# A first group loaded in parts, and a masked maximum taken in one pass: a graph attention layer with pre-normalisation on one core

## The reference

```python
def reference(x, adj, Wq, bq, Wk, bk, Wv, bv, beta):       # x 64x128x384, adj 64x128x128, W 384x384
    h = maximum(layernorm(x), 0)
    q, k, v = heads(h @ Wq + bq), heads(h @ Wk + bk), heads(h @ Wv + bv)      # 12 heads of 32
    scores = q @ k.T / sqrt(32) + beta * adj
    scores = where(adj > 0, scores, -9e15)
    return x + merge(softmax(scores) @ v)
```

## Time and profile before

| | us |
|---|---|
| median of 3 runs | 582.98 (582.75 to 583.28) |
| the profiled execution, its own time | 582.67 |
| its span, first to last instruction | 580.9 |
| PE busy | 552.8 (95%) |
| DVE busy | 469.2 (81%) |
| ACT busy | 464.4 (80%) |
| POOL busy | 115.6 (20%) |

### The profile page before, as it was taken

One profiled execution on the slowest core, in us unless ns is written; L12 is line 12 of the kernel. 1 busy time (PEld: TensorE's weight loads), 2 busy tenths in 40 slices (PEclk: granted clock), 3 DMA queues, 4 the chain that ended last, 5 costly groups with the idle time before them and its releaser, 6 DMA issues.

```text
span 580.9 us, 16356 instructions
## 1 busy us (share of the span) xinstructions
PE 552.8 (95%) x5664; PEld 470.1 (81%) x5664; DVE 469.2 (81%) x803; ACT 464.4 (80%) x1861; POOL 115.6 (20%) x200
## 2 busy tenths in 40 slices
PE   1999999999999999999999999999999999999873
PEld 1778888888888888888888888888888888888662
DVE  5778898888888888889888888988888898777771
ACT  4258889888888988888888888888888889887884
POOL 2201211222121121222112112221211212111111
PEclk9999999999999999999999999999999999999997
DMA  8120120300212020021202112120211200000001
GB/s 287 47 74 16 46 82 16 101 29 32 81 45 68 27 92 35 32 81 42 71 27 80 44 34 81 37 76 27 67 46 45 81 32 30 28 29 29 15 33 37
DMA packets 28429, 31.71 MB, mean 55 GB/s; under 512 B 2544, under 2 KB 28400, under 8 KB 28400
## 3 DMA queue, kind: packets, MB, share of 16 engines
q1 hardware_dynamic: 28400, 31.34, 16.4%
HBM read 18.75 MB, written 12.58 MB: 54 GB/s over the span
## 4 chain that ended last, share of the span: by engine, by line
PE 92%; DVE 2%; issue 2%; ACT 1%; POOLq 0%; POOL 0%
PE G_ps L503 35%; PE S_ps L564 18%; PE PT_ps L548 15%; PE S_ps L523 10%; PE PT_ps L534 8%; PE S_ps L574 3%; PE PT_ps L554 3%; DVE probs L438 2%; ACT probsT L297 1%; ACT probs L289 0%; POOLq L44 0%; DVE h_lo L372 0%; POOL y L264 0%; DVE qk L401 0%; DVE y L448 0%
## 5 line engine op out<-in xcount | busy, mean ns | idle before, releaser
L289 ACT ACTIVATE probs<-probs,negmax 128x128 f32<-128x128 f32 x768 | 298.4, 401 | 0.0
L297 ACT COPY probsT<-PT_ps 128x512 f32<-128x512 f32 x192 | 111.9, 587 | 83.6 <-PE PT_ps L548 81.9
L289 ACT ACTIVATION_READ_ACCUMULATOR probs<-probs,negmax 128x1 f32 x768 | 153.2, 200 | 0.0
L264 POOL TENSOR_TENSOR y<-y,x_ring 128x384 f32<-128x384 f32 x64 | 65.2, 1019 | 312.7 <-DVE y L448 312.7
L503 PE MATMUL G_ps<-h_hi,w_hi 128*128 128x512 f32 x288 | 118.6, 412 | 3.1 <-DVE h_lo L372 3.1
L548 PE MATMUL PT_ps<-ident,probs 128*128 128x128 f32 x768 | 117.5, 277 | 2.5 <-ACT probs L289 1.7
L503 PE MATMUL G_ps<-h_hi,w_lo 128*128 128x512 f32 x288 | 118.5, 411 | 0.0
L503 PE MATMUL G_ps<-h_lo,w_hi 128*128 128x512 f32 x288 | 117.2, 407 | 0.0
L452 DVE TENSOR_REDUCE negmax<-probs 128x12 f32<-128x1536 f32 x64 | 111.6, 1743 | 0.1
L438 DVE TENSOR_TENSOR probs<-S_ps,bias 128x1536 f32<-128x1536 f32 x64 | 109.1, 1705 | 2.2 <-PE S_ps L523 2.2
L548 PEld LDWEIGHTS PT_ps<-ident,probs 128*128 128x128 f32 x768 | 88.1, 140 | 13.0 <-ACT probs L289 3.2
(11 more groups left out here) (36 smaller groups left out, 617.0 us busy)
## 6 DMA issues: line engine op xcount, KB each, us to landing
x_ring<-in_x_dram SPq DMA_DIRECT2D x16, 768.0 KB, 4.7
out_dram<-y SPq DMA_DIRECT2D x64, 192.0 KB, 1.8
adj_in<-in_adj_dram SPq DMA_DIRECT2D x16, 256.0 KB, 2.8
w_raw<-in_L_gnn_Wq_dram SPq DMA_DIRECT2D x1, 576.0 KB, 5.7
w_raw<-in_L_gnn_Wk_dram SPq DMA_DIRECT2D x1, 576.0 KB, 6.7
w_raw<-in_L_gnn_Wv_dram SPq DMA_DIRECT2D x1, 576.0 KB, 7.8
bv_rows<-in_L_gnn_bv_dram SPq DMA_DIRECT2D x1, 192.0 KB, 6.8
bq_raw<-in_L_gnn_bq_dram SPq DMA_DIRECT2D x1, 1.5 KB, 7.1
```

The source lines that it names most:

```text
L264: nc.gpsimd.tensor_tensor(y[:, z.s % 2, :], y[:, z.s % 2, :], x_ring[:, bass.ds(at, D)], ALU.add).then_inc(y_ready, 1)
L289: last = nc.scalar.activation(p, p, ACT.Exp, bias=negmax[:, e, j * KC + m:j * KC + m + 1], accum_out=rowsum[:, e, m * HC + j:m * HC + j + 1])
L297: nc.scalar.copy(probsT[:, m, :], PT_ps[:, m % 2, :]).then_inc(pT_stored[m], 1)
```

## The change

Group 0's x comes in four DMAs, Wq in two (the first 128 columns ahead of the third graph), and Wk and Wv are issued behind the constants and group 1's x. The rounded copies and remainders of the weights are made by unit; all remainders but the first unit's are made on POOL. On DVE a graph's normalisation stands after the next graph's moments. `low_part` of the slots with T but no P stands ahead of `moments`. PE multiplies the identity by itself into a free bank ahead of each of the first transposes. In the slots with P but no A, PE's `transpose_xhat` stands at the end of the slot. The scores, the mask term and beta change sign, so that the mask and the negated maximum become one instruction per head, twelve to a graph, with y after them; `values` waits for the first three of them, `transpose_xhat` for the first six.

```diff
+TURN = -1.0
+MASK_ORDER = [1, 0, 2, 3]
+WARM = [8, 2, 2, 2, 4]
@@ SP
-            sp.dma_start(x_ring[:, 0:GROUP * D].rearrange("p (s d) -> p s d", s=GROUP), x_v[:, 0, :, :]).then_inc(x_loaded[0], 16)
-            for c, w in enumerate((wq, wk, wv)):
-                sp.dma_start(w_raw[:, :, c * D:(c + 1) * D], w.rearrange("(k p) n -> p k n", p=P)).then_inc(w_loaded[c], 16)
+            for q in range(2):
+                load_first(q)
+            load_weights(0, wq, 0, P, w_first)
+            for q in range(2, GROUP):
+                load_first(q)
+            load_weights(0, wq, P, D, w_loaded[0])
...
             sp.dma_start(x_ring[:, GROUP * D:2 * GROUP * D].rearrange("p (s d) -> p s d", s=GROUP), x_v[:, 1, :, :]).then_inc(x_loaded[1], 16)
+            load_weights(1, wk, 0, D, w_loaded[1])
+            load_weights(2, wv, 0, D, w_loaded[2])
@@ POOL
+            def weights_low(first, last):
+                pool.wait_ge(w_hi_ready, min(last, QK_UNITS + 1))
+                ws = slice(first * P, last * P)
+                nc.gpsimd.tensor_tensor(w_lo[:, :, ws], w_raw[:, :, ws], w_hi[:, :, ws].bitcast(F32), ALU.subtract).then_inc(w_lo_ready, 1)
...
+                    weights_low(1, 2)
+                    weights_low(2, 3)
+                if z.static and z.P and z.groups(0) == 0:
+                    if z.s < GROUP - 1:
+                        weights_low(KC + z.s, KC + z.s + 1)
+                    else:
+                        weights_low(QK_UNITS, 3 * KC)
@@ ACT
-                    act.wait_ge(negmax_ready, z.e + 1)
+                    act.wait_ge(masked, z.e + 1)
...
-                    last = nc.scalar.activation(p, p, ACT.Exp, bias=negmax[:, e, j * KC + m:j * KC + m + 1],
+                    last = nc.scalar.activation(p, p, ACT.Exp, bias=negmax[:, e, j * KC + m:j * KC + m + 1], scale=TURN,
@@ DVE
-                        for w in group:
-                            normalise(w)
-                        weights_low(0)
+                            if w.s > 0:
+                                normalise(group[w.s - 1])
+                        normalise(group[-1])
+                        first_weights_low()
...
-                    nc.vector.tensor_tensor(probs[:, a, :, :, :], S_ps[:, :, 0:KC * N].rearrange("p j (m k) -> p j m k", m=KC),
-                                            bias[(z.par + 1) % 2][:, z.s, :].unsqueeze(1).unsqueeze(1).broadcast_to([P, HC, KC, N]),
-                                            ALU.add).then_inc(masked, 1)
+                    dve.wait_ge(scores_in_psum, z.a + 1).then_inc(mask_begun, 1)
+                    for j, signal in zip(MASK_ORDER, (masked_one, masked_two, None, masked)):
+                        for m in range(KC):
+                            last = nc.vector.tensor_tensor_reduce(probs[:, a, j, m, :], S_ps[:, j, m * N:(m + 1) * N], bias[(z.par + 1) % 2][:, z.s, :],
+                                                                  1.0, LARGEST, ALU.add, ALU.min, negmax[:, a, j * KC + m:j * KC + m + 1])
+                        if signal is not None:
+                            last.then_inc(signal, 1)
...
-                    dve.wait_ge(masked, z.a + 1)
-                    nc.vector.tensor_reduce(negmax[:, a, :], probs[:, a, :, :, :].rearrange("p j m k -> p (j m) k"), axis=AX.X,
-                                            op=ALU.max, negate=True).then_inc(negmax_ready, 1)
...
+                if z.T and not z.P:
+                    low_part(z)
                 if z.L:
...
-                if z.T:
+                if z.T and z.P:
                     low_part(z)
@@ PE
-                pe.wait_ge(masked, z.a + 1)
+                pe.wait_ge(masked_one, z.a + 1)
...
+            def warm(count):
+                for _ in range(count):
+                    nc.tensor.matmul(G_ps[:, 1, 0:P], ident[:, :], ident[:, :], start=True, stop=True)
...
                 if z.T and not z.P:
+                    warm(WARM[z.s])
                     transpose_xhat(z)
+                    if z.s == GROUP - 1:
+                        warm(WARM[GROUP])
...
-                if z.T and z.P:
+                if z.T and z.A:
                     transpose_xhat(z)
                 if z.E:
                     transpose_probs(z, 2)
                 if z.P:
                     for part in STRETCH_2[z.s]:
                         project(z, *part)
+                if z.T and z.P and not z.A:
+                    transpose_xhat(z)
```

More of the change, by code:

```diff
@@ L9 @@
 ACT = mybir.ActivationFunctionType
-AX = mybir.AxisListType
 HEADS = 12
@@ L15 @@
 MASKED = -9.0e15
+LARGEST = 3.4028234663852886e38
+TURN = -1.0
+MASK_ORDER = [1, 0, 2, 3]
 RING = 4
@@ L63, in gnn_attention @@
         beta_col = sb("beta_col", [P, 1])
+        beta_turned = sb("beta_turned", [P, 1])
         minus_half = sb("minus_half", [P, 1])
@@ L101, in gnn_attention @@
         consts_set = sem("consts_set")
-        w_hi_ready, w_lo_ready = sem("w_hi_ready"), sem("w_lo_ready")
-        bq_ready = sem("bq_ready")
+        w_first = sem("w_first")
+        w_hi_ready, w_lo_first, w_lo_ready = sem("w_hi_ready"), sem("w_lo_first"), sem("w_lo_ready")
+        bq_ready, beta_ready = sem("bq_ready"), sem("beta_ready")
+        x_first = [sem(f"x_first{i}") for i in range(GROUP)]
         x_loaded = [sem(f"x_loaded{i}") for i in range(2)]
@@ L113, in gnn_attention @@
         v_in_psum, v_stored = sem("v_in_psum"), sem("v_stored")
-        scores_in_psum, masked, negmax_ready = sem("scores_in_psum"), sem("masked"), sem("negmax_ready")
+        scores_in_psum, mask_begun = sem("scores_in_psum"), sem("mask_begun")
+        masked_one, masked_two, masked = sem("masked_one"), sem("masked_two"), sem("masked")
         probs_ready = [sem(f"probs_ready{m}") for m in range(KC)]
@@ L202, in _, with load_first, load_weights @@
         def _(sp):
-            sp.dma_start(x_ring[:, 0:GROUP * D].rearrange("p (s d) -> p s d", s=GROUP), x_v[:, 0, :, :]).then_inc(x_loaded[0], 16)
-            for c, w in enumerate((wq, wk, wv)):
-                sp.dma_start(w_raw[:, :, c * D:(c + 1) * D], w.rearrange("(k p) n -> p k n", p=P)).then_inc(w_loaded[c], 16)
+            def load_first(q):
+                sp.dma_start(x_ring[:, q * D:(q + 1) * D], x[q, :, :]).then_inc(x_first[q], 16)
+            def load_weights(c, w, first, last, landed):
+                sp.dma_start(w_raw[:, :, c * D + first:c * D + last], w.rearrange("(k p) n -> p k n", p=P)[:, :, first:last]).then_inc(landed, 16)
+            for q in range(2):
[4 more added lines that the diff above has]
+            load_weights(0, wq, P, D, w_loaded[0])
             with nc.allow_non_contiguous_dma(reason="bias columns, once"):
@@ L271, in _, with weights_high @@
         def _(act):
[L273 to L278, removed]
+            def weights_high(first, last):
+                act.wait_ge(w_first if last == 1 else w_loaded[first // KC], 16)
+                ws = slice(first * P, last * P)
+                nc.scalar.copy(w_hi[:, :, ws], w_raw[:, :, ws]).then_inc(w_hi_ready, 1)
+            weights_high(0, 1)
             def exponentials(z, m):
@@ L305, in store_qk @@
                     nc.scalar.activation(qk[z.par][:, u, :], G_ps[:, u % 2, :], ACT.Identity, bias=bq_scaled[:, u:u + 1],
-                                         scale=SCALE).then_inc(qk_stored_act, 1)
+                                         scale=TURN * SCALE).then_inc(qk_stored_act, 1)
                 else:
@@ L338, in slot @@
                         store_qk(z, u)
+                if z.static and z.T and not z.P and z.s == 1:
+                    weights_high(1, 2)
                 if z.static and z.T and not z.P and z.s == GROUP - 1:
-                    weights_high(2)
+                    weights_high(2, 3)
                     act.wait_ge(const_loaded, 64)
-                    nc.scalar.mul(bq_scaled[:, :], bq_raw[:, :], SCALE).then_inc(bq_ready, 1)
+                    nc.scalar.mul(bq_scaled[:, :], bq_raw[:, :], TURN * SCALE).then_inc(bq_ready, 1)
                     act.wait_ge(bq_ready, 1)
+                    weights_high(3, 4)
+                if z.static and z.P and z.groups(0) == 0 and z.s < GROUP - 1:
+                    if z.s < 2:
+                        weights_high(KC + 1 + z.s, KC + 2 + z.s)
+                    else:
+                        weights_high(QK_UNITS, 3 * KC)
             slots(act, slot)
@@ L348, in _, with first_weights_low @@
         def _(dve):
[L349 to L352, removed]
+            def first_weights_low():
+                dve.wait_ge(w_hi_ready, 1)
+                nc.vector.tensor_tensor(w_lo[:, :, 0:P], w_raw[:, :, 0:P], w_hi[:, :, 0:P].bitcast(F32), ALU.subtract).then_inc(w_lo_first, 1)
             def moments(q, at, s):
@@ L380, in mask_terms @@
                     dve.wait_ge(bias_ready, z.count(0))
-                nc.vector.tensor_scalar(mask_term[:, :], adj_in[z.par][:, z.s, :], 0.0, MASKED, ALU.is_le, ALU.mult).then_inc(mask_ready, 1)
```

(24 more changed lines are left out.)

3 lines of the change are left out of this document (1 added, 2 removed).

## The result

| us | before | after |
|---|---|---|
| median (runs) | 583.13 (4) | 592.91 (4), 591.93 to 593.49 |
| span of the profiled execution | 580.9 | 590.9 |
| first mask, second mask | 32.99, 39.89 | 32.81, 39.41 |
| first mask of the last group | 540.47 | 550.65 |
| from there to the end of the span | 40.4 | 40.3 |

A forecast was written before the change was run, and what follows sets the result against it. PE holds nearly all of the chain, so only the ends can win. First projection -4.0, clock -2.5, moved transposes +2.1, last group +0.4 sum to -4.0 against 582.67: 578.7 us, range 573.5 to 587.

The forecast's parts named there:

- It fits, with 0.15 us to spare: nothing won, nothing lost.: Loop's full slots: with y after twelve masks PE may go on after 3.98 us and comes there after 4.13.
- Rival B: Full slots: at 0.298 us a mask instruction y comes too late, +12.8 us, 595.5 in all; chance 0.22.
- The mask instruction: DVE's mask pass: 0.263 us per instruction, 3.16 for twelve; ends 0.198 and 0.298.
- rival A: Mask pass: the minimum costs nothing extra, 0.198 us each, last four slots 3.00 for 3.68; 575.6; chance 0.20.
- the tail: Last group's four slots: PE needs 3.78 us where it took 3.68, costing 0.4 in all.
- The start: Kernel's beginning: first projection -4.0, clock -2.5, moved transposes +2.1 us.
- The first projection: Start of PE's projections: at 11.0 instead of 14.98, 4.0 us earlier; the other end 13.2, a gain of 1.8.
- The clock: First projection matmuls on PE: identity products bring the later pace of 0.234 us each, gaining 2.5; ends 0 and 2.5.
- The moved transposes: First projected group, slot end: stores queue behind rounding and remainder, costing 0.25, 0.5 and 1.35, together 2.1 us.
- At nothing: POOL's remainders, later Wk and Wv, the signs, beta's product and extra waits were taken to cost nothing.

The follow-up runs named there:

- mask-only: The kernel before with only the new twelve-instruction mask pass, the old start kept: 594.28 us, ratio 1.0192.
- start-only: Also called start alone: the changed kernel with the old mask (one addition, one reduction) and the whole new start: 583.36 us, ratio 1.0011.
- written-out: The changed kernel with all groups written out, no loop on any engine: 582.22 us, ratio 0.9994.
- moved by 56 instructions: The changed kernel with 112 already met waits (56 instructions) at the head of DVE's program: 594.78 us, ratio 1.0216.
- by 130: The changed kernel with 260 already met waits (130 instructions) at the head of DVE's program: 601.95 us, ratio 1.0327.
- the one of 284: The kernel before with the mask as twelve plain additions and the one old reduction: 620.75 us, ratio 1.0649.
- 100 apart: The kernel before with 200 already met waits (100 instructions) at the head of DVE's program, its body unchanged: 588.09 us, ratio 1.0085.
- tile last: The new start with the old mask, and beta's new one-column tile allocated last: 581.44 us, ratio 0.997.
- the best one: Changed kernel: DVE's slots written out, beta's tile last, POOL's last weight remainders single, last rounded copies earlier, transposes mid-slot except slot 0: 579.52 us, ratio 0.9933.
- the kernel without identity products: The tile last kernel without the identity products on PE: 583.5 us, ratio 1.0002.
- 220: The kernel before with one instruction of the new mask kind added per slot, old mask kept: 587.04 us, ratio 1.0073.

## Why the prediction was wrong

**The step that failed** is the loop's, where I wrote "It fits, with 0.15 us to spare: nothing won, nothing lost." It costed the mask in time on DVE and not in instructions of the loop's body. With a body of 380 in place of 196 each jump back leaves DVE idle for 2.35 to 2.6 us, 1.8 of which reach PE, 9.1 in five jumps. The mask-only kernel has the stalls, the start-only and the written-out one do not, and length alone, without the new instruction, brings them. No rival held this. Rival B ended on the right side but named another mechanism, y too late in every slot, and that is refuted: y had 0.79 us to spare. Its 595.5 lies near the measured 592.91 by chance. The question I didn't ask of the diff was how many instructions the engine that closes a loop turn must issue; the trace of before could have asked it for me, since nothing in it bounds what a longer body does at a jump, and I gave that no end of a range.

What the idle time is made of isn't shown. The runs only say what an explanation has to fit: it comes at the jump of a long body and not without a loop; the body of 380 has it at each of its three places (12.4 us in five stalls, 11.9 moved by 56 instructions, 12.7 by 130), the one of 284 as much (11.8); the one of 196 has it at neither of its two places, 100 apart; and ACT, with 283 instructions, did not stall.

**The mask instruction**, taken at 0.263 us with ends of 0.198 and 0.298, measured 0.21. The readout is an instruction of its own (0.08 us long), as rival B feared, but runs beside the next one, so rival A had nearly the right price: 2.54 us for twelve. That most outputs of a running value need a second instruction was my assumption: here the sums of the exponentials and the minima of the new mask have one, the plain reductions none. And the 0.96 elements per ns in the lower end stood without a row; the kernel before shows 0.95 between the 1,152 elements of a weight remainder, 1.27 us from start to start, and the 384 of `low_part`, 0.465; between the mask's 1,536 (1.61) and the 128 of the plain additions (0.19) it is 0.99. DVE before:

```profile
10.16 1.35 DVE L352 TENSOR_TENSOR w_lo<-w_raw,w_hi 128x1152 fp32r<-128x1152 f32 x1
11.43 1.48 DVE L372 SCALAR_TENSOR_TENSOR h_lo<-S_ps,h_hi 128x384 fp32r<-128x384 f32 x3
```

Rival A's gain in the last group did not come all the same: PE goes on 3.44 us after the scores (3.68 before), not 3.00, since the first mask starts 0.20 behind them and not 0.02, and the four transposes behind y take 0.64 in place of 0.45. A slot is 7.11, 0.05 less than before, so **the tail**, +0.4, came out at -0.2.

**The start** was to bring the first mask 4.4 us forward (-4.0 - 2.5 + 2.1); in after it came 0.2 earlier. **The first projection**, 4.0 earlier, came 1.9 earlier, at 13.10: my other end was 13.2. Graph 2's x landed at 6.43, where I had put graph 3 at 6.0, and the last normalisation took 1.14 us in place of 0.47, with POOL's weight remainder (9.51, 0.99 us) beside it. I had counted that remainder "at nothing".

**The clock** term, 2.5, came in six profiled executions (start alone, written out, tile last, the best one and the two of after moved), where the first matmuls stand 0.23 apart, and was worth 2.1 by the kernel without identity products. In after's profiled execution the first thirteen took 4.85 us, 0.6 less than without identity products and 1.5 more than in start alone: they stand 0.43 apart until 16.5 us, at a granted clock of 0.72 and 0.71. The granted clock alone doesn't tell the pace: before (below) and without identity products they stand 0.43 apart too, in start alone 0.23, all three at a granted clock of 1.00 (start alone and the kernel without products read from 12 to 18 us). That PE is at a lower level of its clock there was my reading of the slower pace; no run shows such a level. The rows have the columns of the earlier trace rows, with the number of instructions behind each busy time:

```profile
12.00:15.00 3.00, 2.11 (x7) 1.53 (x7) 1.92 (x6) 0.86 (x3) 1.76 (x4) 0.72 1.08 373
15.00:18.00 3.00, 3.00 (x12) 2.35 (x11) 1.43 (x6) 0.00 (x0) 1.80 (x3) 0.71 1.11 334
```

PE before:

```profile
15.57 0.63 PE L503 MATMUL G_ps<-h_hi,w_lo 128*128 128x512 f32 x1
16.00 0.63 PE L503 MATMUL G_ps<-h_lo,w_hi 128*128 128x512 f32 x1
```

How often after's slower start at a granted clock of 0.72 happens is open; the eleven runs of start alone spread from 581.49 to 584.65.

**The moved transposes**, 2.1, cost 1.7, read in the written-out kernel: 0.08 ahead of unit 2 (0.25 predicted), 0.48 ahead of unit 5, which waits for the store of unit 3 (0.71 from start to start in place of 0.23; 0.5 predicted), and 1.16 ahead of the first scores (1.35 predicted). In after the last was 1.8, because `bias` held DVE (below). PE's timeline:

```profile
24.83 0.39 PE L569 MATMUL G_ps<-h_lo,w_hi 128*128 128x512 f32 x1
25.54 0.47 PE L569 MATMUL G_ps<-h_hi,w_hi 128*128 128x512 f32 x1 [0.32 <-ACT qk L362]
...
29.37 1.16 PE L589 MATMUL S_ps<-qk 32*128 32x128 f32 x24 [1.17 <-DVE h_lo L433]
```

The mechanism, stores queued behind rounding and remainder, was as predicted.

**At nothing** were two things that had a price. POOL's remainders held DVE: 2.79 us for `bias`, whose chain piece of 2.20 stands where 0.3 should, and 1.14 for a normalisation; in the best version, where no remainder stands beside it, `bias` took 0.32 at the same place. And beta's product, costed as one instruction, brought a tile: 0.11 us a group, some 1.6 in all.

## What to carry to other kernels

Before one long instruction inside a hardware loop is split into many short ones, count the instructions of the loop's body on that engine as well as their time; here, on DVE, 220 were free and 284 were not, and it was enough to write the loop out for that engine alone. The number is DVE's: ACT's 283 were free, so look at the trace of the engine in question. Look at the first idle interval behind the loop's line, once per turn, and not only at a typical slot. Allocate a small new tile last, so that the timing of everything else stays comparable.

## What the runs showed of the hardware

- A jump back in a loop of 284 to 380 instructions on DVE leaves it idle for 2.18 to 2.60 us; with 196 (in two positions, 100 apart) and 220 there was no such idle time. On ACT a loop body of 283 has none: 0.47 us from start to start across the jump.
- A tile start moved by 32 bytes, off a multiple of 64, lengthens PE's work by 0.11 us in 34.04 with the same instructions (start alone against tile last). Why isn't shown.
- A DVE instruction that reads only SBUF can stand for as long as POOL's own does: in after, `bias` 2.79 us beside 2.65 (0.32 in the best version, with no remainder beside it), a normalisation 1.14 in place of 0.47, beside 0.99. One that reads PSUM was not held: in the best version 0.56 us inside POOL's 1.97. What holds the one and not the other isn't shown. From the best version's timelines:

```profile
28.15 1.97 POOL L308 TENSOR_TENSOR w_lo<-w_raw,w_hi 128x384 fp32r<-128x384 f32 x2
```

```profile
28.50 0.56 DVE L439 SCALAR_TENSOR_TENSOR h_lo<-S_ps,h_hi 128x384 fp32r<-128x384 f32 x1 [0.99 <-ACT h_hi L377]
```

- A wait that is met costs DVE time when there are many: with 56 instructions of waits at its head DVE's first work came at 7.0 us, with 130 at 14.7: 74 more for 7.7 us, which is 0.10 each.
